# Gathering the convolution's rows and edge attributes by tiles into a ring of 28 slots, in a three-layer SAGE network with an edge-gated convolution

## The reference

```python
# three times (relu but for the last):
mean = segment_sum(h[src], dst) / clip(count, 1)
h = mean @ Wl[i] + bl[i] + h @ Wr[i]
x1 = layernorm(x + h)
# the convolution
z = concatenate([x1[dst], x1[src], edge_attr])
msg = sigmoid(z @ Wf.T + bf) * softplus(z @ Ws.T + bs)
agg = segment_sum(msg, dst)
agg = (agg - mean_0(agg)) * rsqrt(var_0(agg) + 1e-5) * bn_gamma + bn_beta
h = relu(layernorm(agg + x1) * ln_gamma + ln_beta)
out = layernorm(x1 + h + x1)
```

## Time and profile before

| | |
|---|---|
| median of 3 runs | 4347.5 us (4346.2 to 4349.9) |
| the profiled execution | 4348.5 us, span 4346.7 us |
| busy, share of the span | PE 57%, DVE 45%, ACT 26%, POOL 70% |
| granted clock of PE, mean | 0.68 |
| bytes moved | 359.8 MB |

### The profile page before, as it was taken

One profiled execution on the slowest core, in us unless ns is written; L12 is line 12 of the kernel. 1 busy time (PEld: TensorE's weight loads), 2 busy tenths in 40 slices (PEclk: granted clock), 3 DMA queues, 4 the chain that ended last, 5 costly groups with the idle time before them and its releaser, 6 DMA issues.

```text
span 4346.7 us, 57254 instructions
## 1 busy us (share of the span) xinstructions
PE 2461.9 (57%) x11955; PEld 2011.2 (46%) x11956; DVE 1967.5 (45%) x4033; ACT 1141.5 (26%) x2171; POOL 3064.0 (70%) x3220
## 2 busy tenths in 40 slices
PE   5444445456444445455444444555688888888870
PEld 4334344446343444445434444445555555555540
DVE  3222222224122222223433433322688888888877
ACT  1000000002000000001000000000588888888864
POOL 4777777776777777775777777777277777777740
PEclk7555555657555555567655555555899999999995
DMA  6222222222222222222333332222344444444420
GB/s 213 53 53 53 53 53 53 53 53 75 53 53 53 53 53 53 53 53 67 111 109 107 112 110 62 53 53 53 93 127 128 127 127 128 127 127 128 127 79 30
DMA packets 292204, 359.81 MB, mean 83 GB/s; under 512 B 174421, under 2 KB 222958, under 8 KB 291887
## 3 DMA queue, kind: packets, MB, share of 16 engines
q0 software_dynamic: 115728, 264.72, 23.0%
q1 hardware_dynamic: 175696, 94.04, 7.5%
q10 hardware_dynamic: 752, 0.74, 0.1%
HBM read 314.20 MB, written 52.19 MB: 84 GB/s over the span
## 4 chain that ended last, share of the span: by engine, by line
POOL 58%; issue 32%; DMA 3%; DVE 3%; PE 2%; POOLq 1%; ACT 1%; ACTq 0%; DVEq 0%; SPq 0%
POOL gath L516 43%; POOL gath L535 15%; DMA gath<-y_dram,idx 2%; DMA y_dram<-work 1%; PE ps L664 0%; ACT work L895 0%; PE ps L771 0%; POOLq L513 0%; PE ps L777 0%; DVE mv L1351 0%; ACTq L820 0%; PE ps L654 0%; DVE st_b L1347 0%; DVE work L1304 0%; DMA acc<-in_xT 0%
## 5 line engine op out<-in xcount | busy, mean ns | idle before, releaser
L516 POOL DMA_INDIRECT gath<-y_dram,idx x2352 | 2219.5, 944 | 791.4 <-issue 721.3
L630 PE MATMUL ps<-gath,work 128*128 x5952 | 1403.8, 417 | 1524.3 <-ACTq L838 1396.5
L630 PEld LDWEIGHTS ps<-gath,work 128*128 128x128 f32 x5952 | 1244.8, 313 | 1683.1 <-issue 1682.9
L1248 DVE TENSOR_TENSOR acc<-acc,ps 128x129 f32 x744 | 215.5, 290 | 2098.6 <-PE ps L630 2049.3
L535 POOL DMA_INDIRECT gath<-q_dram,idx x832 | 818.7, 984 | 263.0 <-issue 252.5
L835 ACT COPY idx<-srcT_sb 128x4 int32 (+1 forms) x579 | 111.7, 193 | 2746.1 <-DMA gath<-y_dram,idx 2180.2
L1231 DVE SCALAR_TENSOR_TENSOR work<-ps,w_of,dstT_sb 128x512 f32<-128x512 f32 x753 | 560.0, 744 | 2.2 <-issue 2.2
L735 PE MATMUL ps<-pq,work 128*128 x1664 | 484.8, 393 | 95.7 <-DVE work L1442 65.0
L735 PEld LDWEIGHTS ps<-pq,work 128*128 128x128 f32 x1664 | 251.0, 191 | 208.4 <-issue 135.2
L1442 DVE TENSOR_TENSOR work<-ps,gath 128x1024 f32<-128x1024 f32 x208 | 253.6, 1219 | 70.2 <-issue 56.3
L1433 DVE TENSOR_TENSOR acc<-acc,ps 128x128 f32 x832 | 236.6, 284 | 93.2 <-PE ps L752 65.2
(11 more groups left out here) (201 smaller groups left out, 1235.2 us busy)
## 6 DMA issues: line engine op xcount, KB each, us to landing
gath<-y_dram,idx POOLq DMA_INDIRECT x2352, 2.5
ea_sb<-ea_parts SPq DMA_DIRECT2D x832, 32.0 KB
ea_parts<-pq SPq DMA_DIRECT2D x128, 196.0 KB, 2.6
gath<-q_dram,idx POOLq DMA_INDIRECT x832, 2.8
y_dram<-work SPq DMA_DIRECT2D x21, 448.0 KB, 3.2
eaT_sorted<-in_eaT SPq DMA_DIRECT2D x2, 3136.0 KB, 19.7
pq<-eaT_sorted SPq DMA_DIRECT2D x16, 392.0 KB, 3.2
q_dram<-work SPq DMA_DIRECT2D x7, 896.0 KB, 4.1
```

The lines of the kernel that those rows point to most:

```text
L516: pool.indirect_dma_start(msg[:, u, 0:F], None, y_dram, bass.IndirectOffsetOnAxis(ap=idx[:, u:u + 1], axis=0)).then_inc(s_quad[q], 16)
L630: last = te.matmul(ps[:, i % OHS, 0:FA], lhsT=oh4[:, i % OHS, u, :], rhs=gath[:, bass.ds(places[i] + u * FA, FA)], start=u == 0, stop=u == ...
```

## The change

The convolution no longer gathers one tile per pair, but each tile once, in 196 quads of four tiles, into a ring of 7 quads (28 slots, `RC * QT`). The same holds for the edge attributes, one load of 128 KB per quad in place of four of 32 KB per group. The pairs find their slot by a table: `regs` now holds the window number, the slot (tile modulo 28) and the number of the tile's quad plus 1.

- SP gives the indices of a quad by a DMA from `srcT_sb` to `idx` (`give_indices`), waits for the landings of edges and rows in order and counts them on `ea_landed` and `q_landed`, waits on `added` until the slot's last pair is done (a row of `q_regs` that DVE now works out as well) and counts `slot_free`.
- POOL waits for the indices and `slot_free` and gathers by quads.
- PE and DVE load 16 window numbers, 16 slots and 4 quad numbers at the head of each turn. DVE's addition of q rows is made in four instructions of 256 columns, each at its pair's slot. PE takes the edge attributes at a register's place too.
- ACT copies no indices any more. `srcs`, `src_sorted`, their 7 gathers, and the transposes and copies for them are gone.
- The ring overlaps `x_sb`. So x1 goes to `x1_dram` by SP, one chunk before each chunk of q, and SP reads it back into x_sb after the last pre addition. POOL's copy is gone. In the tail the doubling on ACT now follows the squares, and DVE's addition of bn_beta follows the centring.
- On DVE the second `schedule` and the new row stand before the signal `q_tab`.

```diff
+RC = 7
-        x_sb = sb("x_sb", [P, NW * F])
+        shared = sb("shared", [P, NW * F + UB * 2 * F])
+        x_sb = shared[:, 0:NW * F]
+        q_ring = shared[:, NW * F + UB * 2 * F - RC * QT * 2 * F:NW * F + UB * 2 * F]
...
@@ sync
             with sp.Fori(0, NCH) as it:
+                sp.wait_ge(s["x1_ready"], it + 1)
+                sp.dma_start(x1_dram[bass.ds(it * (CW * P), CW * P), :].rearrange("(u p) f -> p u f", p=P), x1c)\
+                    .then_inc(s["x1_sent"], 16)
+                sp.wait_ge(s["x1_sent"], (it + 1) * 16)
+                sp.sem_inc(s["x_kept"], 1)
                 sp.wait_ge(s["q_staged"], (it + 1) * 4 + 2)
...
+            def conv_quad(m, q, first, last):
+                if not (first and q == 0):
+                    sp.wait_ge(s_ea[(q - 1) % RC], (m if q == 0 else m + 1) * 16)
+                    sp.sem_inc(s["ea_landed"], 1)
+                if not (first and q < 2):
+                    sp.wait_ge(s_quad[(q - 2) % RC], (m if q < 2 else m + 1) * (QT * 16) + SAGE_LANDED)
+                    sp.sem_inc(s["q_landed"], 1)
+                if not (last and q >= RC - 2):
                     alone(sp)
+                    give_indices((q + 2) % RC, m * (RC * QT) + (q + 2) * QT)
+                if not first:
+                    sp.wait_ge(s["added"], done_regs[q])
+                    sp.sem_inc(s["slot_free"], 1)
+                alone(sp)
+                give_edges(q, m * (RC * QT * P) + q * QT * P)
...
+            sp.wait_ge(s["added"], NS + G * GB)
+            x1v = x1_dram.rearrange("(w p) f -> p w f", p=P)
+            for w0_, w1_ in ((0, NW // 2), (NW // 2, NW)):
+                sp.dma_start(xs[:, w0_:w1_, :], x1v[:, w0_:w1_, :]).then_inc(s["x1_back"], 16)
...
@@ gpsimd
-            with pool.Fori(0, NCH) as it:
-                pool.wait_ge(s["x1_ready"], it + 1)
-                gp.tensor_copy(chunk(x_sb, it, F), x1c).then_inc(s["x_kept"], 1)
-            with pool.Fori(0, NG // GB) as m:
-                for g in range(GB):
-                    pool.wait_ge(s["qi"], m * GB + g + 1)
+            with pool.Fori(0, NQ // RC) as m:
+                for q in range(RC):
+                    pool.wait_ge(s_ix[q], m * 16 + 16)
+                    pool.wait_ge(s["slot_free"], m * RC + q + 1)
                     alone(pool)
-                    for t in range(G):
+                    for u in range(q * QT, (q + 1) * QT):
                         pool.indirect_dma_start(
-                            qg[:, g, t, :], None, q_dram,
+                            q_ring[:, u * 2 * F:(u + 1) * 2 * F], None, q_dram,
...
@@ tensor
             def load_windows(first):
-                pe.reg_load(w_regs, regs[0:1, bass.ds(first + NC * P, UB)])
+                pe.reg_load(w_regs, regs[0:1, bass.ds(first, UB)])
+                pe.reg_load(e_regs, regs[0:1, bass.ds(first + NC * P, UB)])
+                pe.reg_load(l_regs, regs[0:1, bass.ds(first + 2 * NC * P, UB)].rearrange("o (g t) -> o g t", t=G)[:, :, G - 1])
+                for g in range(GB):
+                    pe.reg_alu(quad_needed[g], l_regs[g], 1, ALU.max)
...
@@ scalar
-            def indices(g, slot):
-                act.wait_ge(s["added"], g + 1)
-                sc.copy(idx[:, slot * G:(slot + 1) * G], srcs[:, bass.ds(g * G, G)]).then_inc(s["qi"], 1)
...
-            for c in range(NCH):
-                sc.mul(chunk(x2, c, F), chunk(x_sb, c, F), 2.0).then_inc(s["x2_ready"], 1)
             for i, w in enumerate(range(0, NW, 4)):
...
+            act.wait_ge(s["x1_back"], 32)
+            for c in range(NCH):
+                sc.mul(chunk(x2, c, F), chunk(x_sb, c, F), 2.0).then_inc(s["x2_ready"], 1)
...
@@ vector
+            def load_slots(first, a, b):
+                dve.reg_load(e_regs[a:b], regs[0:1, bass.ds(first + NC * P, b - a)])
+                n = (b - a) // G
+                dve.reg_load(a_regs[0:n], regs[0:1, bass.ds(first + 2 * NC * P, b - a)].rearrange("o (g t) -> o g t", t=G)[:, :, G - 1])
+                for g in range(n):
+                    dve.reg_alu(quad_needed[g], a_regs[g], 1, ALU.max)
+                return [dve.snap(r, min_val=0, max_val=RC * QT - 1) for r in e_regs[a:b]]
...
-                    dve.wait_ge(s_qg[(slot - 2) % GB], (turn + 1) * 64)
+                    dve.wait_ge(s["q_landed"], quad_needed[at])
...
-                    v.tensor_tensor(pre[:, slot % 2, :, :], ps_pre[:, slot % 2, :, :], qg[:, (slot - 2) % GB, :, :],
-                                    ALU.add).then_inc(s["added"], 1)
+                    for t in range(G):
+                        last = v.tensor_tensor(pre[:, slot % 2, t, :], ps_pre[:, slot % 2, t, :],
+                                               q_ring[:, bass.ds(slots[at * G + t] * (2 * F), 2 * F)], ALU.add)
+                    last.then_inc(s["added"], G)
...
             with dve.Fori(1, NG // GB) as m:
                 wins = load_windows(m * UB - UB)
+                slots = load_slots(m * UB - 2 * G, 0, UB)
```

More of the change, by code:

```diff
@@ L196, in build_gnn @@
         tabT = work[0:3 * NC, 9344:9344 + P].bitcast(i32)
[L197 removed]
+        q_tabT = work[0:6 * NIC, 9472:9472 + P].bitcast(i32)
         diag_w = work[:, 5768:5768 + NIC * P].rearrange("p (c n) -> p c n", n=P)
@@ L257, in build_gnn @@
         s_quad = [sem(f"s_quad{q}") for q in range(RQ)]
-        s_qg = [sem(f"s_qg{g}") for g in range(GB)]
-        s_ea = [sem(f"s_ea{g}") for g in range(GB)]
+        s_ea = [sem(f"s_ea{g}") for g in range(RC)]
+        s_ix = [sem(f"s_ix{g}") for g in range(RC)]
+        SAGE_LANDED = 3 * (NQ // RQ) * QT * 16
         LOADS = 6
@@ L425, in _ @@
             sp.wait_ge(s["tab_back"], 32)
[L426 to L429, removed]
[L430 to L436 removed]
+            sp.wait_ge(s["q_tab_back"], 32)
@@ new lines, in _, with needed @@
+            give_indices(0, 0)
+            give_indices(1, QT)
+            for q in range(RC):
+                conv_quad(0, q, True, False)
+            def needed(m):
+                sp.reg_load(n_regs, q_regs[0:1, bass.ds(m * RC + (5 * NIC * P - RC), RC)])
+                for q in range(RC):
+                    sp.reg_alu(done_regs[q], n_regs[q], 0, ALU.max)
+                    sp.reg_alu(done_regs[q], done_regs[q], G * GB, ALU.add)
+            with sp.Fori(1, NQ // RC - 1) as m:
+                needed(m)
+                for q in range(RC):
+                    conv_quad(m, q, False, False)
@@ L636, in conv_columns @@
                 pe.wait_ge(s["res_kept"], NCH * 2)
-                for c in range(2 * NC):
-                    rows = d_rowsf if c < NC else s_rowsf
-                    last = te.transpose(ps_rows[:, c, :], rows[:, c % NC * P:(c % NC + 1) * P], ident[:, :])
+                for c in range(NC):
+                    last = te.transpose(ps_rows[:, c, :], d_rowsf[:, c * P:(c + 1) * P], ident[:, :])
                 last.then_inc(s["rows_tr"], 1)
@@ L959, in conv_step @@
                     sc.activation(log_, log_, ACT.Ln, bias=1.0).then_inc(s["logd"], 1)
-                if ok(j + 2) and ok(j):
-                    indices(j + 2, (slot + 2) % GB)
                 if ok(j):
@@ L1420, in ok, with conv_step @@
                 return not isinstance(g, int) or 0 <= g < NG
-            def conv_step(j, slot, m, wins):
+            def conv_step(j, slot, m, wins, slots, at):
                 def add_sum(t):
@@ L1489, in _ @@
             N4 = -(-NW // 4)
+            for c in range(NCH):
+                dve.wait_ge(s["x2_ready"], c + 1)
+                v.tensor_tensor(chunk(x_sb, c, F), chunk(x_sb, c, F),
+                                bn_sb[:, 1, :].unsqueeze(1).to_broadcast([P, CW, F]), ALU.add).then_inc(s["xb_ready"], 1)
             dve.wait_ge(s["sq_used"], N4)
```

123 lines of the change are left out of this document (73 added, 50 removed).

## The result

The changed kernel takes 4590.43 us (median of 4 runs, 4589.32 to 4592.22) against 4347.19 before: a ratio of 1.0543, 95% interval 1.0499 to 1.0587. It is slower by 243 us. Forecast were 4613 us and a range of 4485 to 4690.

What follows compares the result with a forecast made beforehand. DVE's instruction stream was taken to set the convolution's turn, with POOL held to it. Terms 153 + 11 + 89 + 2 + 2 + 1 + 7 = 265 us on 4348.5 gave about 4613 us, range 4485 to 4690.

Steps and rivals of the forecast that it cites:

- (a): Register loads and range checks at the head of DVE's turn: 3.0 us a turn, bounds 2.3 and 3.5, 153 us.
- (c): PE's longer pause at the head lowers its clock: 1.75 us a turn, 89 us, bounds 0 and 163.
- (b): DVE's addition L1442 in four pieces: 0.22 us at each head, swallowed inside the turn; 11 us, bounds 0 and 120.
- (d): Around the convolution's loop: first gather +2 us, last turn's short loads +2, the x1 stage +1.
- (e): Tail: DVE's seven additions to x_sb wait for ACT's doubling behind the last square, +7.1 us; reading x1 back hidden.
- (f): Taken at nothing: ACT's index copies, edge loads on SP, seven gathers fewer, queue table 3 us later (3 if uncovered).
- The clock holds: Rival: PE's pause once a turn does not lower its clock, the 89 us fall away: 4525 us, chance 0.22.
- The gathers lead: Rival: DVE's loads overlap its work, POOL's gathers set the convolution's pace, the change is faster: 4278 us, chance 0.12.
- New signals bind: Rival: SP's landing signals come late each quad, 80 us more, 4690; chance 0.08 for signals or dearer pieces.

Runs made afterwards that it cites:

- a_fill: The changed kernel with three unneeded matmuls of 128x512 added at the end of PE's turn, in PE's pause: 4537.6 us, ratio 1.0418 to the kernel before.
- a_one_add: The changed kernel with DVE's addition of gathered rows in one instruction on a fixed place of SBUF, slots unread: 4583.3 us, ratio 1.0524 to the kernel before.
- a_split_half: The changed kernel with both engines' register loads spread over the groups and two gathers for a quad instead of four: 4338.9 us, ratio 0.9963 to the kernel before.

## Why the prediction held, and where it did not

The total was 20 us too high (4613 for 4590; 265 us for 243). By its steps:

- **(a) Loads, 3.0 us a turn.** Right: DVE's idle time at the head grew by 4.31 - 1.12 = 3.19. The strided load, taken at 1.0 for bounds of 0.4 and 1.0, measured 0.955. By the Trainium skill's figure (Runtime: NRT & Kernel Launch, Instruction fetch mechanics) the estimate would have been 4.0; the trace agrees with about 200 ns a register for the strided load (0.24) and for the eight that start at an odd place, and not for sixteen in a row (0.07). The page speaks of loads from HBM; these come from SBUF. "Nothing hides it" held, and so did the sentence in (c) that PE's pause "still lies beside DVE's 3.0": in a_fill PE keeps its loads and DVE does not wait for it.
- **(b) Pieces, 0.22 at the head, nothing inside.** Right: from the first piece to L1499 are 1.33 us where L1442 took 1.14, +0.19, and groups inside the turn went from 4.97 to some 5.01. The heads as a whole, with the last turn's, came to 174 us for the 153 + 11 + 2 of (a), (b) and (d).
- **(c) Clock, 1.75 a turn, 89 us.** The mechanism was right and the term was mis-sized: 1.08 us (a_fill), 56 in all. What was wrong in it is the slack. I took 2.15 us of PE's time lost, and 2.14 were; I took 0.4 us of it as covered before DVE waits, and 1.06 were. That the 2.15 fits so well is partly luck: it is an average of turns with a short slow part (1.4 to 1.7 us lost) and turns with a long one (2.7 to 3.1), and I had one size in mind. This term is 31 to 33 us too high, more than the 20 us of the total; the heads (8 us over their terms) and the other groups (4 us, taken at nothing) took part of it back.
- **(d) Start.** +3.3 in all for 3 forecast, and that is luck: 2.8 of them lie before the last sum of the SAGE layers. From there to the first product it took 89.9 us and now 90.3, so the stage of x1 and the start gave 0.4. The last turn's short loads gave 1.9 of the 2 forecast.
- **(e) Tail, +7.1.** Right: the additions stand behind the last square, and the reduction L1561 starts 7.2 us after PE's last product of squares has ended (4480.81 to 4488.03), where L1491 followed it at once. That only +4.1 is left behind the last product comes from PE: its two rounds of sums took 12.3 and 11.5 us where they took 13.5 and 13.1. No term had this.
- **(f) At nothing.** The covers held, as far as can be told. That includes the table of the SAGE items, the one with a price of 3 us: the gathers of the second layer began at 1053.9 us, before the change at 1054.2. The 2.8 us at the last sum of the layers arose later. L565 was busy for 4.4 us more than L516 (2223.9 for 2219.5 us) at the same count of gathers, and a_one_add, with the same table, was 0.7 us ahead of the kernel before.
- **The range.** With (a) and (c) both at their upper bounds the sum is 4713, not 4690, and the upper bound of (b) is 122, not 120. Nothing came of either.
- **Rivals.** "The clock holds" falls with 0.91. "The gathers lead" asked for 208 groups without head, 4.76 us each. Spread loads gave them without head but at 5.03 us, with half of the gathers, and the convolution was then 24.5 us shorter than before the change; the 82 us of that rival need shorter groups too. "New signals bind" falls with a_split_half, which keeps them all, for chips where rows land in time.

## What to carry to other kernels

Registers loaded at the head of the loop stopped both engines that loaded them, so each engine's head has to be costed by itself, and with it how much later that engine may come before another waits for it. Here PE had 1.06 us of such slack: it swallowed half of what the lowered clock took from PE, and it is also all that a shorter head on DVE alone could have gained at the full clock, so both heads were shortened. Load the registers instead some at a time, for later use, behind an instruction that runs for over a microsecond, where the sequencer was free. An average over turns can hide two kinds of turn: look at the turns one by one before a cost is read from it. And an experiment whose added load nothing reads measures nothing: count the instructions in its trace first.

## What the runs showed of the hardware

- The sequencer of DVE works on while a long instruction runs: a load of eight (0.60 us) behind a product of 1.22 us left the group at 5.03 us. At the head of the turn, behind a product of 0.68 us, three loads were exposed.
- Four numbers at a stride (0.955 us on DVE, 0.996 on PE) cost more than eight in a row (0.60, at a place that is a multiple of eight).
- Of pauses of PE of 2.50 us once a turn, 24 of 51 brought the lower clock; 4.35 us did in all 51; 1.30 us did in none. With 2.7 of the 4.35 us filled, so that 1.75 stayed, it was at 1.00.
- On two of the four chips that the experiments came to, indirect gathers landed so late that the unchanged kernel took 23 to 25% longer, at the same issue time for each gather.
